# A decoder layer on one core: attention numerator with the key-value sums stationary, and x transposed by the DMA queue

## The reference

```python
q_phi = (exp(q @ orf.T / 2 - |q|^2 / 8) + 1e-6) / 8       # x @ Wq.T + bq, split into heads; k_phi likewise
kv   = einsum('bhlm,bhld->bhmd', k_phi, v)
ksum = sum(k_phi, axis=2)
out  = einsum('bhlm,bhmd->bhld', q_phi, kv) / einsum('bhlm,bhm->bhl', q_phi, ksum)[..., None]
x    = layernorm(x + out @ Wo.T + bo)
# then: x = layernorm(x + softmax cross-attention on the context)
#       x = layernorm(x + ternary-weight gated MLP with per-row rounding of its inputs)
```

## Time and profile before

| | |
|---|---|
| three runs, us | 568.69, 572.29, 567.56 (median 568.69) |
| the profiled execution, us | 565.91 |
| its span | 564.2 |
| mean granted TensorE clock | 0.943 of full speed |
| busy: PE, DVE, ACT, POOL, us | 486.1, 472.4, 411.2, 387.6 |
| PE's weight loads, us | 345.5 |

### The profile page before, as it was taken

One profiled execution on the slowest core, in us unless ns is written; L12 is line 12 of the kernel. 1 busy time (PEld: TensorE's weight loads), 2 busy tenths in 40 slices (PEclk: granted clock), 3 DMA queues, 4 the chain that ended last, 5 costly groups with the idle time before them and its releaser, 6 DMA issues.

```text
span 564.2 us, 17426 instructions
## 1 busy us (share of the span) xinstructions
PE 486.1 (86%) x5932; PEld 345.5 (61%) x5990; DVE 472.4 (84%) x1380; ACT 411.2 (73%) x811; POOL 387.6 (69%) x768
## 2 busy tenths in 40 slices
PE   3056999999999998999999999999999998977651
PEld 2034766677667676777777777777777776654320
DVE  0784565889999998999999999999999998998671
ACT  0226667778888887888888888888888887867531
POOL 7032665677777777788777777788788876665432
PEclk9576999999999999999999999999999999998765
DMA  5604776566877775556565656566555587473111
GB/s 142 221 0 82 138 133 110 87 122 122 135 131 133 132 125 110 125 124 131 117 130 120 130 118 130 119 129 124 121 125 123 124 124 122 87 113 67 41 45 37
DMA packets 192649, 64.14 MB, mean 114 GB/s; under 512 B 172384, under 2 KB 192352, under 8 KB 192608
## 3 DMA queue, kind: packets, MB, share of 16 engines
q1 hardware_dynamic: 190080, 60.46, 55.3%
q10 hardware_dynamic: 2528, 3.15, 1.7%
HBM read 17.31 MB, written 4.19 MB: 38 GB/s over the span
## 4 chain that ended last, share of the span: by engine, by line
PE 60%; DVE 12%; DMA 9%; ACT 7%; issue 4%; SPq 4%; POOL 4%; ACTq 0%; POOLq 0%; DVEq 0%
PE bank L1084 9%; PE bank L1151 8%; PE bank L1274 5%; DMA hqT<-hq 5%; PE bank L1244 5%; PE bank L1297 4%; PE bank L1167 3%; PE bank L1104 3%; PE bank L1149 3%; PE bank L1133 2%; PE bank L1099 2%; PE bank L1181 2%; PE bank L1261 2%; DMA tT<-nmT 2%; PE bank L1224 1%
## 5 line engine op out<-in xcount | busy, mean ns | idle before, releaser
L1084 PE MATMUL bank<-wq_hi,xT 128*128 128x512 f16 (+1 forms) x256 | 71.7, 336 | 0.9 <-ACT xT L511 0.7
L1151 PEld LDWEIGHTS bank<-kvm,phq 128*128 128x128 f32 x512 | 62.2, 192 | 2.5
L1151 PE MATMUL bank<-kvm,phq 128*128 128x34 f32 x512 | 59.8, 272 | 0.0
L416 POOL TENSOR_TENSOR pkA<-qk,pkA 128x512 f16<-128x512 f32 x32 | 37.6, 1176 | 31.7 <-ACT pkA L511 31.6
L466 POOL TENSOR_TENSOR xq<-xm,nmagic 128x256 bf16<-128x256 f32 x32 | 19.6, 613 | 51.5 <-DVE xm L911 51.5
L430 POOL TENSOR_TENSOR rs<-ve,mhalf 128x1 f32<-128x1 f32 x96 | 52.9, 552 | 0.0
L865 DVE TENSOR_REDUCE negm<-bank 128x4 f16<-128x512 f32 x64 | 43.8, 685 | 8.6 <-PE bank L1200 8.5
L555 ACT ACTIVATE x<-y,nmr,rs 128x256 f32<-128x256 f32 x64 | 38.3, 599 | 11.1 <-DVE y L976 9.7
L915 DVE SCALAR_TENSOR_TENSOR g<-th,bank 128x512 f32<-128x512 f32 x64 | 43.2, 676 | 3.7 <-ACT th L643 3.6
L1244 PE MATMUL bank<-pT,ctxv 128*32 128x128 f32 x1024 | 42.4, 284 | 4.5 <-ACT pT L620 4.3
L511 ACT ACTIVATE pkT<-bank 128x512 f16<-128x512 f32 x32 | 19.1, 597 | 37.0 <-PE bank L1181 37.0
(11 more groups left out here) (180 smaller groups left out, 1611.5 us busy)
## 6 DMA issues: line engine op xcount, KB each, us to landing
xs<-in_x_dram SPq DMA_DIRECT2D x32, 128.0 KB, 2.5
xr<-in_x_dram SPq DMA_DIRECT2D x32, 128.0 KB, 2.2
cs<-in_ctx_dram SPq DMA_DIRECT2D x32, 128.0 KB, 2.2
out_dram<-ot SPq DMA_DIRECT2D x32, 128.0 KB, 1.9
ffn_ld<-in_L_ffn_w_gate_dram ACTq DMA_DIRECT2D x1, 1024.0 KB, 5.5
ffn_ld<-in_L_ffn_w_up_dram ACTq DMA_DIRECT2D x1, 1024.0 KB, 8.7
ffn_ld<-in_L_ffn_w_down_dram ACTq DMA_DIRECT2D x1, 1024.0 KB, 10.5
pkAT<-pkA SPq DMA_TRANSPOSE x64, 3.2
```

The lines of the kernel that those rows point to most:

```text
L1084: last = T.matmul(o, xT[:, 2 * part + c, :], w[:, c, cols], start=(n == 0), stop=(n == 5))
L1151: last = T.matmul(at_num[:, 2 * DV * k:2 * DV * (k + 1)], phq[:, par, k, :], kvm[:, k, :, :].rearrange("p h d -> p (h d)"), start=False, s ...
```

## The change

The numerator is turned round. `nump` now has, for each pair of heads, the key-value sums as stationary operand (128x32 f32) and the query features as moving operand (128 columns), once for the values and once for the denominators, which the ones of `vv` now give sixteen times over; four such products lie side by side in PE's column groups. The result stands transposed in a whole bank, so `aTp`, the copy `aT` and `att` go; `rd` takes the reciprocal of 2x128 columns in place of 16, and `at` writes `attT`. The epsilon is added to the query features by a new GpSimd step `phe` of 1024 columns, at lag 3 behind `hq0` and ahead of `rs1`; `nump` waits for it. `kvm_` moves from DVE (one masked product) to ACT behind `thi` (two copies of 64 partitions). `xTp` and the copy `xT_` go; a DMA transpose on SyncE's queue writes a double-buffered `xT`, behind `tT_` in the list. Five GpSimd copies and roundings (`xhi`, `chi`, `xqf`, `hq0`, `hq1`) are `tensor_scalar` instead of `tensor_tensor`.

```diff
 # SyncE
+            def xT_(t, par):
+                wait_ahead(sp, t, ("xlo", 0), ("vm", -2))
+                transpose(xT[:, par, :, :], xpk[:, :, :].rearrange("p n d -> p (n d)"), "xT", par)
                 go(tT_, i, par, 5)
+                go(xT_, i, par, 0)
                 go(load_r, i, par, 3)
 # GpSimd
+            def phe(t, par):
+                wait_ahead(pool, t, ("ephq1", 0), ("ephq0", 0))
+                g.tensor_scalar(phq[:, par, :, :], phq[:, par, :, :], PHI_EPS, 1.0, ALU.add, ALU.mult).then_inc(
+                    done["phe"], 1)
-                g.tensor_tensor(hq[:, 0, :], hm[:, 0, :], nmagic[:, :].to_broadcast([P, 512]),
-                                ALU.add).then_inc(done["hq0"], 1)
+                wait_ahead(pool, t, ("hm0", 0))
+                g.tensor_scalar(hq[:, 0, :], hm[:, 0, :], 1.0, -MAGIC, ALU.mult, ALU.add).then_inc(done["hq0"], 1)
                 go(hq0, i, par, 9)
+                go(phe, i, par, 3)
                 go(rs1, i, par, 5)
 # ACT
-            def aT(t, par): ...
-            def xT_(t, par): ...
+            def kvm_(t, par):
+                wait(act, "kvp", t)
+                for e in range(2):
+                    half = slice(64 * e, 64 * e + 64)
+                    last = sc.activation(kvm[half, :, :, e, :],
+                                         at_kv[half, :].rearrange("p (c n d) -> p n c d", n=2, d=DK), ACT.Copy)
+                last.then_inc(done["kvm"], 1)
                 go(thi, i, par, 5)
+                go(kvm_, i, par, 3)
 # DVE
-                v.reciprocal(rden[:, :], heads[:, :, DK]).then_inc(done["rd"], 1)
+                v.reciprocal(rden[:, :, :], at_num[:, 2 * P:].rearrange("p (g t) -> p g t", g=2)).then_inc(done["rd"], 1)
-                v.tensor_tensor(att[:, :, :], heads[:, :, 0:DK],
-                                rden[:, :].unsqueeze(2).to_broadcast([P, H, DK]), ALU.mult).then_inc(done["at"], 1)
+                v.tensor_tensor(attT[:, :, :], at_num[:, 0:2 * P].rearrange("p (g t) -> p g t", g=2), rden[:, :, :],
+                                ALU.mult).then_inc(done["at"], 1)
 # PE
-                T.matmul(at_num, epsc[:, :], kvm[:, :, :, :].rearrange("p c h d -> p (c h d)"), start=True, stop=False)
-                for k in range(PAIRS):
-                    last = T.matmul(at_num[:, 2 * DV * k:2 * DV * (k + 1)], phq[:, par, k, :],
-                                    kvm[:, k, :, :].rearrange("p h d -> p (h d)"), start=False, stop=(k == PAIRS - 1))
+                wait(pe, "phe", t)
+                for n in range(2):
+                    for k in range(PAIRS):
+                        j, at0 = k % 4, 2 * P * n + P * (k // 4)
+                        last = T.matmul(at_num[32 * j:32 * j + 32, at0:at0 + P],
+                                        kvm[:, n, k, :, :].rearrange("p e d -> p (e d)"), phq[:, par, k, :],
+                                        start=True, stop=True)
```

More of the change, by code:

```diff
@@ L223, in decoder_kernel @@
         ).split()}
-        moved = {name: [sem(f"s_{name}{i}") for i in range(2)] for name in ("qT", "kT", "cT", "tT", "hqT", "row")}
+        moved = {name: [sem(f"s_{name}{i}") for i in range(2)] for name in ("qT", "kT", "cT", "tT", "hqT", "row", "xT")}
         def wait_moved(eng, name, t, par, off=0):
@@ L240, in wait, with wait_ahead @@
                 eng.wait_ge(done[name], v)
-        def wait_ahead(eng, t, *producers):
+        def wait_ahead(eng, t, *producers, queues=()):
             counts = [t + off + 1 for _, off in producers]
             counts = [v if isinstance(v, int) else eng.to_reg(v) for v in counts]
+            bytes_in = [v if isinstance(v, int) else eng.to_reg(v) for _, v in queues]
             eng.wait_ge(ids, 3)
+            for (semaphore, _), v in zip(queues, bytes_in):
+                if not isinstance(v, int) or v > 0:
+                    eng.wait_ge(semaphore, v)
             for (name, _), v in zip(producers, counts):
@@ L378, in _ @@
             g.memset(ctxv[:, :, :, DK:DV], 1.0).then_inc(masks, 1)
-            g.memset(vv[:, :, :, DK:DV], 1.0).then_inc(masks, 1)
+            g.memset(vv[:, :, :, DK:32], 1.0).then_inc(masks, 1)
             g.affine_select(out=mask8[:, :], in_=mask8[:, :], compare_op=ALU.is_ge, fill=0.0, base=0,
                             pattern=[[-DK, 8]], channel_multiplier=1).then_inc(masks, 1)
-            g.affine_select(out=kvmask[:, :, :, :], in_=kvmask[:, :, :, :], compare_op=ALU.is_ge, fill=0.0, base=0,
-                            pattern=[[0, PAIRS], [-64, 2], [0, DV]], channel_multiplier=1).then_inc(masks, 1)
             g.memset(pkC[:, :, 2, 0:1], 1.0).then_inc(masks, 1)
-            pool.wait_ge(masks, 5)
+            pool.wait_ge(masks, 4)
             g.affine_select(out=mask8[:, :], in_=mask8[:, :], compare_op=ALU.is_ge, fill=0.0, base=DK - 1,
                             pattern=[[DK, 8]], channel_multiplier=-1).then_inc(masks, 1)
-            g.affine_select(out=kvmask[:, :, :, :], in_=kvmask[:, :, :, :], compare_op=ALU.is_ge, fill=0.0, base=63,
-                            pattern=[[0, PAIRS], [64, 2], [0, DV]], channel_multiplier=-1).then_inc(masks, 1)
-            pool.wait_ge(masks, 7)
+            pool.wait_ge(masks, 5)
             pool.wait_ge(b_in, 64)
             def xhi(t, par):
[L396 to L399, removed]
+                before = (par - 1) % 2
+                wait_ahead(pool, t, queues=((x_in[par], t * 8 - par * 8 + 16),
+                                            (moved["xT"][before], (t - 1 - before) * 8 + 16)))
+                g.tensor_scalar(xpk[:, 0, :], xs[:, par, :], 1.0, 0.0, ALU.mult, ALU.add).then_inc(done["xhi"], 1)
             def xlo(t, par):
@@ L449, in chi @@
             def chi(t, par):
-                landed(pool, c_in, t, par)
-                wait_moved(pool, "cT", t, par, -1)
+                before = (par - 1) % 2
+                wait_ahead(pool, t, queues=((c_in[par], t * 8 - par * 8 + 16),
+                                            (moved["cT"][before], (t - 1 - before) * 8 + 16)))
                 c3 = cs[:, par, :].rearrange("p (h d) -> p h d", h=H)
-                g.tensor_tensor(pkC[:, :, 0:2, :], c3.unsqueeze(2).to_broadcast([P, H, 2, DK]),
-                                onesf[:, 0:1].unsqueeze(2).unsqueeze(3).to_broadcast([P, H, 2, DK]),
-                                ALU.mult).then_inc(done["chi"], 1)
+                g.tensor_scalar(pkC[:, :, 0:2, :], c3.unsqueeze(2).to_broadcast([P, H, 2, DK]), 1.0, 0.0,
+                                ALU.mult, ALU.add).then_inc(done["chi"], 1)
             def clo(t, par):
@@ L463, in xqf @@
             def xqf(t, par):
-                wait(pool, "qnt", t)
-                g.tensor_tensor(xq[:, par, :], xm[:, par, :], nmagic[:, :].to_broadcast([P, D]),
-                                ALU.add).then_inc(done["xqf"], 1)
+                wait_ahead(pool, t, ("qnt", 0))
+                g.tensor_scalar(xq[:, par, :], xm[:, par, :], 1.0, -MAGIC, ALU.mult, ALU.add).then_inc(done["xqf"], 1)
             def hq0(t, par):
-                wait(pool, "hm0", t)
-                g.tensor_tensor(hq[:, 0, :], hm[:, 0, :], nmagic[:, :].to_broadcast([P, 512]),
-                                ALU.add).then_inc(done["hq0"], 1)
+                wait_ahead(pool, t, ("hm0", 0))
+                g.tensor_scalar(hq[:, 0, :], hm[:, 0, :], 1.0, -MAGIC, ALU.mult, ALU.add).then_inc(done["hq0"], 1)
             def hq1(t, par):
-                wait(pool, "hm1", t)
-                g.tensor_tensor(hq[:, 1, :], hm[:, 1, :], nmagic[:, :].to_broadcast([P, 512]),
-                                ALU.add).then_inc(done["hq1"], 1)
+                wait_ahead(pool, t, ("hm1", 0))
+                g.tensor_scalar(hq[:, 1, :], hm[:, 1, :], 1.0, -MAGIC, ALU.mult, ALU.add).then_inc(done["hq1"], 1)
             def iteration(i, par):
@@ L592, in ephk1 @@
                 features(phk[:, PAIRS:H, 0:M], at_phk1, "ephk1", PAIRS)
-            def aT(t, par):
-                wait(act, "aTp", t)
-                copy(attT[:, :, :], at_aT.rearrange("p (c t) -> p c t", c=2), "aT")
+            def kvm_(t, par):
[5 more added lines that the diff above has]
+                last.then_inc(done["kvm"], 1)
             def x1T_(t, par):
@@ L1000, in iteration @@
                 go(v_, i, par, 1)
-                go(kvm_, i, par, 3)
                 go(ad3, i, par, 9)
@@ L1068, in _, with project @@
             orf_pair = orfp[:, :, :].rearrange("p h m -> p (h m)")
[L1070 to L1079, removed]
+            def project(o, cols, par, name):
                 n = 0
@@ L1083, in project @@
                     for part, w in ((0, wq_hi), (0, wq_lo), (1, wq_hi)):
-                        last = T.matmul(o, xT[:, 2 * part + c, :], w[:, c, cols], start=(n == 0), stop=(n == 5))
+                        last = T.matmul(o, xT[:, par, 2 * part + c, :], w[:, c, cols], start=(n == 0), stop=(n == 5))
                         n += 1
@@ L1088, in qkm @@
             def qkm(t, par):
```

(18 more changed lines are left out.)

37 lines of the change are left out of this document (9 added, 28 removed), and 4 rows, old and new, of the table done.

## The result

The changed kernel takes 684.25 us (median of 4, 683.52 to 686.39) against 569.44 of the kernel before: a ratio of 1.202, 95% interval 1.196 to 1.208. I had forecast 637, and 660 as the upper end.

The account below looks back on a forecast made before the run. PE's list was taken to bound the kernel, DVE 0.6 us behind. A loop through `phe` of 17.4 us for 26 iterations added 70.8, the ramp took 3: span 632, with 1.7 around it 634, as median 637; range 590 to 660.

Parts of the forecast that it names:

- The reciprocal: DVE's `rd`, grown from 16 to 256 columns: 1.93 us, +1.75 over now; bounds +0.15 to +2.0.
- d: Duration of the new GpSimd step `phe` of 1024 columns: 1.2 us chosen, between 0.95 and 2.1.
- the three waits behind it: POOL idle 2 us and more before `phe`, DVE some 1.8 before `y2`, ACT idle before `x1_`.
- DVE works in order to the end of `m0`: Loop's first piece, from `y2`'s start through DVE's list: 11.37 us now, 12.40 after the change.
- my loop: Once an iteration from `y2` over `m0`, `g0`, `th0`, `ephq0`, `phe`, `rs1`, `ya2` to `y2`: 16.2 + d = 17.4 us.
- ACT by its list's length alone: ACT's 12.46 us busy plus a standing of d + 1.2 before `x1_`: some 14.9 us, shorter than the loop.
- The clock: Rival: PE at its lower level costs up to 0.6 us more an iteration, 653; forecast including this case 0.74.
- The ramp: Four iterations before the full pipeline: PE's shorter list counts in part, `phe` takes some back, -3 us in all.
- the forecast span of 632: Span 564.2 + 68 = 632 us; 634 with the 1.7 around it, 637 as a median of runs.
- Uncovered it costs 0.7 an iteration: DMA queue: x's transpose delays `hqT_` by up to 0.7 us before `dn`; covered by shorter PE, taken as nothing.
- Only DVE counts: Rival: `phe`'s wait is passed on nowhere, DVE's list alone sets 15.6 us an iteration, some 590; chance 0.10.
- the reciprocal streams: Rival: `rd` on DVE is cheap by the column, the loop is 15.8 us, some 595; chance 0.08.

Follow-up runs that it names:

- The filler: Eight useless f32 transposes added on PE, where it stands idle before `x1Tp`, against the changed kernel: 662.9 us, ratio 1.168 to the kernel before.

## Why the prediction was right or wrong

- *The reciprocal.* Right in kind: 1.75 us whole, 1.67 from its start to the next (391.51 to 393.18), where 1.93 was taken from 1 and 16 columns. That is 6.3 ns a column and not 7.3; it lay within the bounds. The estimate of 2.13 us, worked out in the prediction from the repeat count of 8 that the Trainium skill gives ("VectorE: DVE Perf Modes", the fixed hardware budget), is too high by a quarter against the 1.67; at the page's clock of 0.96 GHz the measured 6.3 ns are an estimated six cycles a column.
- *phe.* d was 1.04, where 1.2 was chosen. Its place and the three waits behind it came out as forecast, and moving one line shows their price.
- *The step that failed* is the first of the loop: "DVE works in order to the end of `m0`", priced as DVE's list without a wait. DVE waits on the way for steps that stand behind `x1_`. Between `y2` and `am` the rows of the kernel before gave 290.63 - 284.93 - 0.35 = 5.35 us:

```profile
290.63 0.41 DVE L892 TENSOR_REDUCE amax<-x 128x1 f32<-128x256 f32 x1
```

In the changed kernel it took 6.05 in a turn at full clock (383.76 to 389.81) and 7.71 in one with PE at the lower level (419.68 to 427.39):

```profile
389.81 0.42 DVE L886 TENSOR_REDUCE amax<-x 128x1 f32<-128x256 f32 x1 [0.27 <-ACT x L554]
```

```profile
424.53 0.42 DVE L783 SCALAR_TENSOR_TENSOR vv<-bank,bqkv 128x256 f32<-128x256 f32 x1 [1.10 <-PE bank L1068]
...
427.39 0.42 DVE L886 TENSOR_REDUCE amax<-x 128x1 f32<-128x256 f32 x1 [0.36 <-ACT x L554]
```

The waits are at `gl1` for `th1` (0.24), at `v_` for `vm` (1.10, in the second kind of turn), at `tlo` for `thi` (0.28, there too) and at `am` for `x2_`. Over the 25 turns from tile 5 to tile 29 the stretch from `y2` to `am` took 6.85 us in the mean, 1.5 over the 5.35. With the measured d and reciprocal my loop would have been 17.0; the mean period was 18.6. So this one step holds nearly all of the loop's miss, the part that the clock adds included. I had named `x1_` as one who waits for GpSimd, and then priced ACT by its list's length alone, 14.9 us ("shorter"). That sum held busy time and one standing, but not the waits that come with it, because PE's `x1Tp` and the steps behind it hang on `x1_`, and `thi` on them. Moreover `x1_` also waits for `ya2` of tile t-2, since x1 has two buffers; I read over that wait in the code. The run with `ya2` first shows that the loop through `x1_` holds the kernel at 17.1 us when `y2` is free.
- *The clock* was mis-sized. The rival said that only `g0` of PE is in the loop and put a cost of at most 0.6 us an iteration on it, without including it in the sum. But `dn`, `vm` and `tm` are in the loop too. On the chain, `dn` took 1.71 us at the lower level where it takes 0.87, and `vm` 1.28 for 0.66. The mean period is 18.6 in place of 17.9. The filler shows it: 21 us less with more work.
- *The ramp.* Forecast -3; the four iterations from `rd` of tile 0 to that of tile 4 took 51.1 us against 41.3 before, three of them at clocks of 0.69 to 0.80. That the loop closes there too, and that PE's shorter list only makes it stand, is my reading; no run tests it.
- *The range.* The largest `d` and reciprocal gave 667, and the range still ended at 660; with the clock's 0.6 us an iteration on top it would have reached 683. That would have been luck, since it put these costs in the wrong places.
- The 50.6 us between the forecast span of 632 and 682.6: 26 x 0.5 = 13 loop, 26 x 0.7 = 18 clock, 13 ramp, and about 6 at the two ends, where the last period took 18.5 instead of 13.3 and the first `rd` came 1.6 later.
- *The DMA transpose.* "Uncovered it costs 0.7 an iteration" is what it cost alone, +19 us; in the changed kernel it does not show, as said. That it sits in a loop of its own with `tlo`, `tT` and `hqT` I had not seen; that 512 columns hold the queue 1.20 us is the upper end of what I had allowed.
- *Only DVE counts* and *the reciprocal streams* were false as forecasts of this kernel. The first is close to what remains when `phe` is moved, 590 against 591.2 measured, in part by luck: its list of 15.6 us has a reciprocal that is 0.26 too long, which stands in for the waits of that run, whose mean period is 15.5.

## What to carry to other kernels

Where every engine works through a list in order, price an added wait by the loops it closes, and follow each of them through every engine that waits in turn; a list's busy time plus one standing is no bound for it. When two loops are of like length, taking a cost out of one shows nothing, so a part's worth can only be read once the other is cut. And before moving work to another engine or queue, look for the spot in its list where it already stands idle: one line of a list was worth 93 us here for GpSimd's step and 27 for the queue's.

## What the runs showed of the hardware

- The granted clock of PE fell to 0.50 of full speed for between three and four us after 2.66 us of standing idle, in an iteration in which PE was busy 14.6 of 19.6 us. It stayed at 1.00 in the one before it, busy 13.1 of 18.0, although PE stood idle 2.67 us there in the same spot. What decides between the two is open here. Filling that idle spot with useless work gave back 21 us.
- A DMA transpose of 512 columns held SyncE's queue 1.20 us, one of 1024 columns 1.25.
- GpSimd's `tensor_scalar` took 0.62 us for 512 columns and 1.04 for 1024, `tensor_tensor` with a broadcast operand 1.04 for 512.
- DVE's reciprocal of 256 columns from PSUM took 1.75 us, 1.67 to the next start, or 6.3 ns a column; in the kernel before, 16 columns took 0.26.
